# Layer 0 of a two-layer graph kernel: one plain float32 matmul for each pair instead of three with rounded parts

## The reference, cut to what matters

```python
def _L0_gnn_ref(x, support, kernel, bias):
    W = support * kernel
    out = jnp.einsum('bnf,nm->bmf', x, W)
    return out + bias

x = _layernorm(x + _L0_gnn_ref(x, adj, adj, L0_gnn_bias), axis=-1)
x = _layernorm(x + _L1_gnn_ref(x, adj, W_lang, W_grav, W_V, W_O, gate_logit, log_sigma), axis=-1)
```

## Time and profile before

| | |
|---|---|
| median of three runs | 680.79 us (680.76 to 680.83) |
| the profiled execution's own time | 681.37 us |
| its span, first to last instruction | 679.6 us |
| TensorE, busy | 666.4 us, 98% |
| VectorE, busy | 506.5 us, 75% |
| ScalarE, busy | 345.6 us, 51% |
| GpSimd, busy | 210.9 us, 31% |
| chain that ended last, on TensorE | 96% |

### The profile page before, as it was taken

How to read it: one execution, slowest core, us unless ns; L and a number is a source line. 1 busy time by engine, 2 the same in 40 slices (tenths; PEclk the granted TensorE clock), 3 DMA queues, 4 the chain that set the end, 5 groups by cost and what they waited for, 6 DMA issues and landing times.

```text
span 679.6 us, 11745 instructions
## 1 busy us (share of the span) xinstructions
PE 666.4 (98%) x3579; PEld 570.7 (84%) x3579; DVE 506.5 (75%) x1523; ACT 345.6 (51%) x614; POOL 210.9 (31%) x454
## 2 busy tenths in 40 slices
PE   8999999999999999999999999999999999999994
PEld 7888888888888888888888888889888888988883
DVE  5935696868869686886959687695968869596886
ACT  4734445464454546455454745545464554545433
POOL 0222315151341515134151513316051432502122
PEclk9999999999999999999999999999999999999997
DMA  7301102011110201111020111102011110001002
GB/s 271 118 6 58 62 32 95 1 62 63 57 68 31 93 0 62 61 62 62 31 93 0 65 58 62 62 31 93 0 69 54 62 62 31 32 0 63 1 31 94
DMA packets 20406, 38.33 MB, mean 56 GB/s; under 512 B 1824, under 2 KB 1824, under 8 KB 20384
## 3 DMA queue, kind: packets, MB, share of 16 engines
q1 hardware_dynamic: 20384, 38.05, 15.1%
HBM read 21.27 MB, written 16.78 MB: 56 GB/s over the span
## 4 chain that ended last, share of the span: by engine, by line
PE 96%; DVE 1%; DMA 1%; ACT 1%; SPq 0%; issue 0%; POOL 0%; POOLq 0%; DVEq 0%
PE ring L357 58%; PE bank_p L377 13%; PE ring L475 4%; PE bank_x L318 3%; PE bank_p L318 3%; PE bank_r L421 3%; PE bank_k L421 3%; PE bank_pt L390 2%; PE bank_r L336 1%; PE bank_pt L336 1%; PE bank_k L336 1%; PE bank_r L397 1%; DMA w_raw<-in_L_gnn_W_lang_dram 1%; PE bank_pt L408 1%; PE bank_x L336 1%; PE bank_x L377 0%
## 5 line engine op out<-in xcount | busy, mean ns | idle before, releaser
L562 ACT ACTIVATE yT_hi<-ring 128x512 fp32r<-128x512 f32 x128 | 76.0, 594 | 109.7 <-PE ring L357 109.5
L357 PE MATMUL ring<-hT_hi,T_hi 128*128 128x512 f32 x320 | 129.2, 404 | 0.0
L357 PE MATMUL ring<-hT_hi,T_lo 128*128 128x512 f32 x320 | 125.3, 392 | 0.0
L357 PE MATMUL ring<-hT_lo,T_hi 128*128 128x512 f32 x320 | 124.8, 390 | 0.0
L777 DVE TENSOR_TENSOR yT_lo<-ring,yT_hi 128x512 fp32r<-128x512 f32 x128 | 87.5, 684 | 31.4 <-ACT yT_hi L562 31.4
L357 PE MATMUL ring<-M_hi,hT_hi 128*128 128x512 f32 x256 | 101.5, 396 | 0.0
L357 PE MATMUL ring<-M_hi,hT_lo 128*128 128x512 f32 x256 | 100.2, 392 | 0.0
L357 PE MATMUL ring<-M_lo,hT_hi 128*128 128x512 f32 x256 | 99.9, 390 | 0.0
L1084 POOL TENSOR_SCALAR z_ve<-z_mv 128x2 f32<-128x2 f32 x32 | 7.0, 219 | 264.8 <-DVE z_mv L873 260.1
L1077 POOL TENSOR_TENSOR x_lo<-x_sb,x_hi 128x512 fp32r<-128x512 f32 x60 | 75.8, 1298 | 22.3 <-ACT x_hi L562 22.3
L777 DVE TENSOR_TENSOR u_lo<-ring,u_hi 128x512 fp32r<-128x512 f32 x64 | 44.3, 692 | 49.1 <-ACT u_hi L562 49.0
(11 more groups left out here) (159 smaller groups left out, 1373.8 us busy)
## 6 DMA issues: line engine op xcount, KB each, us to landing
x_sb<-in_x_dram SPq DMA_DIRECT2D x15, 1024.0 KB, 5.4
out_dram<-o_sb SPq DMA_DIRECT2D x60, 256.0 KB, 2.0
x_sb<-in_x_dram SPq DMA_DIRECT2D x2, 512.0 KB, 5.4
w_raw<-in_L_gnn_W_lang_dram SPq DMA_DIRECT2D x1, 1024.0 KB, 6.6
o_sb<-in_L_gnn_W_grav_dram SPq DMA_DIRECT2D x1, 1024.0 KB, 9.5
h_sb<-in_L_gnn_W_V_dram SPq DMA_DIRECT2D x1, 1024.0 KB, 11.7
w_raw<-in_L_gnn_W_O_dram SPq DMA_DIRECT2D x1, 1024.0 KB, 8.3
out_dram<-x_sb SPq DMA_DIRECT2D x4, 256.0 KB, 2.0
```

The lines of the kernel that those rows point to most:

```text
L357: last = pe.matmul(bank[:, :], a, b, start=n == 0, stop=n == len(terms) - 1)
L562: return act.activation(dst, src, ACT.Copy, scale=scale)
```

## The change

Layer 0 multiplies `x_sb` by `mix` in plain float32, one matmul a pair. The rounding of x, on ScalarE, GpSimd and (for group 0) VectorE, and that of the mixing matrix are gone, with `x_hi`, `x_lo`, `mix_hi` and `mix_lo`. x has two buffers. `layer0(g, h)` now does two pairs in one call, with the waits of both ahead of the first and one report behind the second. TensorE's and SyncE's loops are written out (`for` in place of `Fori`).

```diff
-        x_sb = sb("x_sb", [R, NP, D])
-        x_hi = sb("x_hi", [R, NP, D], fp32r)
-        x_lo = sb("x_lo", [R, NP, D], fp32r)
+        x_sb = [sb(f"x_sb{i}", [R, NP, D]) for i in range(2)]
...
-            sp.wait_ge(x_lo_done, NP)
-            sp.dma_start(x_sb[:, :, :], x_v[1]).then_inc(x_loaded, 16)
+            load_x(1, x_loaded[1])
 
             def load(g):
 
-                sp.wait_ge(x_lo_done, NP * g)
-                sp.dma_start(x_sb[:, :, :], x_v[g]).then_inc(x_loaded, 16)
+                sp.wait_ge(l0_done, NP * g - NP)
+                load_x(g, x_loaded[g % 2])
...
-            with sp.Fori(1, NG - 2, 1) as g:
+            for g in range(1, NG - 2):
                 load(g + 2)
                 store(g - 1)
...
-            def layer0(g, p):
-                pe.wait_ge(x_lo_done, NP * g + p + 1)
-
-                if p >= 2:
-                    pe.wait_ge(y_added, NP * g + p - 1)
-                elif p == 1 and not (isinstance(g, int) and g < 2):
+            def layer0(g, h):
+                if g == 0:
+                    pe.wait_ge(x0_loaded[h], 16)
+                else:
+                    pe.wait_ge(x_loaded[g % 2], 16 * ((g + 1) // 2))
+
+                if h:
+                    pe.wait_ge(y_added, NP * g + 2)
+                elif g >= 2:
                     pe.wait_ge(p_copied, 2 * g - 2)
-                bank = (bank_x, bank_p)[p % 2]
-                for n, (w, r) in enumerate(parts(mix_hi, mix_lo, x_hi, x_lo)):
-                    last = pe.matmul(bank[:, :], w[:, :], r[:, p, :], start=n == 0, stop=n == 2)
-                last.then_inc(l0_done, 1)
+                for a in range(2):
+                    last = pe.matmul((bank_x, bank_p)[a][:, :], mix[:, :], x_sb[g % 2][:, 2 * h + a, :], start=True,
+                                     stop=True)
+                last.then_inc(l0_done, 2)
...
-            with pe.Fori(2, NG - 2, 2) as g:
+            for g in range(2, NG - 2, 2):
                 step(g, 0)
                 step(g + 1, 1)
...
-            def split_x(g, p):
-                pool.wait_ge(x_hi_done, 2 * g + p // 2 - 1)
-                pool.tensor_tensor(x_lo[:, p, :], x_sb[:, p, :], x_hi[:, p, :], ALU.subtract).then_inc(x_lo_done, 1)
```

More of the change, by code:

```diff
@@ L79, in bass_two_layer_graph_resnorm @@
         mix = sb("mix", [R, R])
-        mix_hi = sb("mix_hi", [R, R], fp32r)
-        mix_lo = sb("mix_lo", [R, R], fp32r)
         bias_bc = sb("bias_bc", [R, D])
@@ L185, in bass_two_layer_graph_resnorm @@
         x0_loaded = [sem(f"x0_loaded{c}") for c in range(2)]
[L186 to L189, removed]
+        x_loaded = [sem(f"x_loaded{i}") for i in range(2)]
         l0_done = sem("l0_done")
@@ L247, in out_rows @@
         def out_rows(g):
-            return x_sb if isinstance(g, int) and g == NG - 1 else o_sb
+            return x_sb[0] if isinstance(g, int) and g == NG - 1 else o_sb
         def kt_bank(g):
@@ L264, in _, with load_x @@
         def _(sp):
-            sp.dma_start(x_sb[:, 0:2, :], x_v[0][:, 0:2, :]).then_inc(x0_loaded[0], 16)
+            def load_x(g, done, t=slice(0, NP)):
+                sp.dma_start(x_sb[g % 2][:, t, :], x_v[g][:, t, :]).then_inc(done, 16)
+            load_x(0, x0_loaded[0], slice(0, 2))
             sp.wait_ge(adj_zeroed, 1)
@@ L271, in _ @@
             sp.dma_start(bias_bc[:, :], bias.partition_broadcast(R)).then_inc(bias_loaded, 16)
-            sp.dma_start(x_sb[:, 2:4, :], x_v[0][:, 2:4, :]).then_inc(x0_loaded[1], 16)
+            load_x(0, x0_loaded[1], slice(2, 4))
             sp.dma_start(gates[:, 0:1], gate_logit.partition_broadcast(R)).then_inc(gates_loaded, 16)
@@ L445, in step @@
                 layer0(g + 1, 0)
-                layer0(g + 1, 1)
                 project(g, par, 8)
@@ L450, in step @@
                     apply_k(g - 1, 3)
-                layer0(g + 1, 2)
-                layer0(g + 1, 3)
+                layer0(g + 1, 1)
                 project(g, par, 9)
@@ L483, in _ @@
                 pe.transpose(bank_r[:, 0:R], ident[:, :], ident[:, :])
-            pe.wait_ge(mix_steps, 5)
+            pe.wait_ge(mix_steps, 3)
             for s in (L, G):
-                layer0(0, 2 * s)
-                layer0(0, 2 * s + 1)
+                layer0(0, s)
                 for i in range(DC):
@@ L562, in copy @@
                 return act.activation(dst, src, ACT.Copy, scale=scale)
[L564 to L575, removed]
             def normalise_h(g, par, p):
@@ L615, in normalise_out, with step @@
                                bias=z_nb[:, p:p + 1]).then_inc(o_ready, 1)
-            def step(g, par, tail=True, ahead=True):
+            def step(g, par, tail=True):
                 hi_proj(g, 0)
@@ L646, in step @@
                     normalise_out(g - 1, 3)
-                if ahead:
-                    split_x(g + 2, 0)
-                    split_x(g + 2, 1)
                 hi_proj(g, 10)
@@ L675, in hi_row @@
                 last.then_inc(setup_hi, 1)
-            split_x0(0)
             hi_weight(0)
-            split_x0(1)
             act.wait_ge(gates_loaded, 32)
@@ L704, in _ @@
             hi_value(M_hi, 3 * DC)
-            split_x(1, 0)
-            split_x(1, 1)
             step(0, 0, tail=False)
@@ L712, in _ @@
                 step(g + 1, 1)
-            step(NG - 2, 0, ahead=False)
+            step(NG - 2, 0)
             g = NG - 1
@@ L938, in _ @@
             dve.tensor_tensor(mix[:, :], mix[:, :], ident[:, :], ALU.add).then_inc(mix_steps, 1)
[L939 to L942, removed]
             def lo_weight(i, first, end):
@@ L1111, in columns, with step @@
                                    ALU.mult).then_inc(floors_ready, 1)
-            def step(g, tail=True, ahead=True):
+            def step(g, tail=True):
                 if tail:
@@ L1119, in step @@
                     scale_y(g + 1, q)
-                if ahead:
-                    for p in range(NP):
-                        split_x(g + 2, p)
                 columns(g, 0)
@@ L1135, in _ @@
                 scale_y(0, q)
-            for p in range(NP):
-                split_x(1, p)
             step(0, tail=False)
@@ L1142, in _ @@
                 step(g)
-            step(NG - 2, ahead=False)
+            step(NG - 2)
             g = NG - 1
```

## The result

| | before | changed |
|---|---|---|
| median, three runs each | 680.79 us | 693.16 us (690.92, 693.16, 693.46) |
| ratio, 95% interval | | 1.017, 1.0156 to 1.0184 |
| median with all later runs (30 of before, 13 of the changed one) | 680.8 us | 691.26 us |
| span of the profiled execution | 679.6 us | 691.2 us |

The kernel is slower, as forecast. The three runs that gave 693.16 are a little unlucky. Four of the changed kernel's 13 executions take 693.1 to 693.5 us, with a mean granted clock of 0.992; the other nine take 690.9 to 691.4, with 0.995 to 0.997. One of the four was profiled, and there TensorE's clock fell to its half level for 3.4 us in the setup; for the other three the fall is inferred from the time and the mean clock. So the change costs 10.5 us between the medians, and about 2 more where the clock falls. The two have to be explained apart.

The account below looks back on a forecast made before the run. TensorE's back-to-back issue was taken as the bound. 31 calls at +0.38 us gave +11.8, everything else 0: 681.37 became 693.2 for the profiled execution, so 692.6 us for the median, range 689 to 700.

Parts of the forecast that it names:

- The bound: Whole run: a step is as long as what TensorE issues; gains on other engines or queues cannot shorten it.
- Four streams: Layer 0's plain float32 matmul: four streams a pair with loads hidden, +0.38 us a call, +11.8 us; chance 0.72.
- The transposes' rows: Plain float32 transposes, four in 0.44 us, 0.109 each: the sign for one stream a pair, not carried over to products.
- The price of a stream: Layer 0's pair: four 512-column streams of 0.216 us plus an instruction's part, taken as 0.89 us, 1.78 a call.
- The 0.012 us by instruction: Fixed part of each matmul beside its columns, from the 512- and 256-column spacings; about 0.012 us.
- The start: Setup: the first call's extra 0.38 us hides in TensorE's 1.6 us wait for the first weight; 0.4 if uncovered.
- The edits at nothing: Removed rounding, merged waits, x's loads with two buffers and written-out loops: each priced at 0 us.
- One stream, or two: Rival in layer 0's matmul: fewer streams a pair, faster, 651.7 us with one or 666 with two; chance 0.07.
- Uncovered loads: Rival in layer 0: stationary loads not hidden, 699.4 us with one a pair, 722 with all four; chance 0.17.
- Instruction fetch: Rival in TensorE's 2.3 times longer stream: one uncovered fetch a step, 65 us, 758 us in all; chance 0.02.
- Three streams: Rival in layer 0's matmul: the engine drops lo times lo, a pair costs the same 0.70 us; chance 0.02.

Follow-up runs that it names:

- `e_again`: The changed kernel run again with no edit: 691.21, 691.36, 691.30, 691.26 us, and 693.11 with a mean clock of 0.992.
- `e_again2`: The changed kernel run once more with no edit: 690.88, 691.03, 691.10, 691.21 us, and 693.23 with a mean clock of 0.992.
- the same filling: Changed kernel plus 16 identity transposes behind layer 0's first call in the setup, run twice: 691.32 us, then 691.91 us.
- the two-stream kernel: Kernel before without the third matmul of each pair, x_hi times mix_lo, which adds zero for these inputs: 667.22 us, ratio 0.9799.
- the filled one: Kernel before without each pair's third matmul, plus 18 identity transposes behind layer 0's first call: 666.60 us, ratio 0.979.

## Why the prediction was right, and where its terms were off

**The bound.** Right: only what TensorE issues counts. The kernel with nothing but the plain matmul changed (and the wait of x's load, which has to follow it) is 10.2 us slower, the whole change 10.5.

**Four streams.** Right as a price: each matmul is two entries of 0.427 us, each as long as two streams. The transposes' rows, which spoke for one stream, were no guide: the same operands as products take 0.223 us against 0.109. The Trainium skill ("FP8 and Floating Point Precision", TensorE Precision Notes) gives true FP32 four passes through the array, and the 0.855 us a pair agree with it. The transpose mode that the Trainium skill names ("TensorE: Matmul & The Clock Gate", Terms), four times faster for FP32, agrees in kind; the factor was 2 here at 128 columns. What holds a transpose at 0.109 us, where one stream of 128 columns is 0.053, is not shown; a float32r matmul of that size is at 0.12 too.

**The price of a stream.** This term was too high: 0.89 us a pair was taken, 0.855 measured. The 0.012 us by instruction, from the difference between 512 and 256 columns of float32r, is not paid between the streams of a plain matmul. A call costs +0.31, not +0.38, and 31 calls 9.6 us, not 11.8.

**What the forecast did not have.** The next step's first call in the chain, before and after, gives the length of a step against the 331.20 of the earlier trace rows and the 337.53 above:

```profile
370.68 0.70 PE bank_x L318 x3
```

```profile
377.67 0.86 PE bank_x L315 x2
```

A step is 40.14 us where it was 39.48, +0.66; two calls give 0.62, and about 0.02 a call lies in the projection behind it, whose first loads come late: the page of the changed kernel has the first kind of matmul behind a call at 445 ns where it was 396, and loads that come 0.42 us apart up to 344.90, in the timeline above, and 0.23 to 0.24 behind it. The row before, and the rows after:

```profile
L357 PE MATMUL ring<-M_hi,hT_hi 128*128 128x512 f32 x256 | 101.5, 396 | 0.0
```

```profile
L355 PE MATMUL ring<-M_hi,hT_hi 128*128 128x512 f32 x256 | 114.0, 445 | 0.0
...
L355 PEld LDWEIGHTS ring<-M_hi,hT_hi 128*128 128x128 f32 x256 | 48.2, 188 | 15.4 <-issue 7.2
```

15 steps at +0.66 are 9.9 us and the call in the setup is 0.3: 10.2. The profiled executions bear this out when they are counted from the start of the first weight's matmuls, which is set by a transfer and differs from one execution to the next. From 10.49 to the end of the span the kernel before takes 669.1 us; the changed one takes 679.2 to 679.3 from 10.05 in `e_again`, from 9.76 in `e_again2` and from 9.80 with only the plain matmul changed. That is +10.1 each time. The 10.5 between the medians has 0.4 more, which is not accounted for; it is no more than the 0.6 by which equal kernels differed here (691.3 and 691.9 with the same filling).

**The start.** The call was to be hidden by a wait of 1.6 us, and was. That it would start earlier was seen and priced at nothing: "the warm-up ends only at 7.1, and after that the first weight's transfer decides". The call did start earlier, at 6.13, 6.73 and 6.45 in the three profiled executions. The removed rounding is not needed for that: with the rounding still in place the two-stream kernel started its call at 6.42 and the filled one at 6.27. The first weight is set by its transfer, as said. What the prediction had no term for is the clock's fall, in 4 of 13 runs. That is why the three-run median, 693.16, lies within 0.6 of the forecast: a term 2.2 us too high and a clock that was not forecast nearly cancel, which is luck. Against 691.26 the forecast is 1.3 us high.

**The edits at nothing.** The rounding, the waits, the loads and the written-out loops were worth nothing, as said. The kernel with only the plain matmul changed, which keeps all of them as they were, shows it for all together, to 0.4 us; the loop has a run of its own. The waits and the loads were not tried one by one, and no row of TensorE's waits names them.

**The rivals.** One stream, or two: refuted by 0.855 us a pair. Uncovered loads: refuted, the load path idles 0.24 us between the loads. Instruction fetch: 0.46 MB instead of 0.18, no effect. Three streams: refuted.

## What to carry to other kernels

When one engine is busy back to back, price every edit in that engine's streamed columns and treat work taken off the others as worth nothing until a wait shows otherwise. A plain float32 product costs four streams of its columns, so it loses to three float32r matmuls whose rounding is hidden, and loses by more, 0.855 us against 0.47 here, where one operand is exact in the rounded type and two matmuls do. A transpose's price says nothing about a product's, even with the same operands. And before one profile's wait is held against another's, the same kernel should be profiled again: one wait at the start was 2.3 us and 1.4 us in the same kernel here.

## What the runs showed of the hardware that was not expected

A plain float32 matmul of 512 columns is recorded as two loads and two matmuls; each entry lasts 0.427 us, which is 1,024 columns at 2.4 GHz to within 1 ns, while a float32r stream of 512 columns takes 0.228 to 0.233, 15 to 20 ns above its 0.213. So four plain streams cost 3.7 of the others, not four. And TensorE fell to 1.2 GHz for some 3.4 us while it was busy back to back, about 1.2 us after an idle stretch of 2.3 us had ended, in one profiled execution of the changed kernel; its other two, with 1.4 us idle, kept the full clock, and so did two other kernels in executions with 2.1 us idle.
